# State-space stage: four batches prepared ahead of the state loop, against one unrolled pipeline

## The reference, cut to what matters

```python
xz = _bound(jnp.einsum('bld,ed->ble', hidden_states, W_in))
x, z = jnp.split(xz, 2, axis=-1)
...
x = _bound(jax.nn.silu(jnp.transpose(xc, (0, 2, 1))))      # xc: causal convolution over 4 tokens, plus conv_b
x_dbl = jnp.einsum('bld,ed->ble', x, W_x)                  # 8 columns dt, 16 columns B, 16 columns C
dt = _bound(x_dbl[..., :DT_RANK])
...
dt = jnp.einsum('blr,dr->bld', dt, W_dt) + b_dt
dt = jnp.clip(jax.nn.softplus(dt), 0.0001, 20.0)
def step(h, inp):
    u_t, dt_t, B_t, C_t = inp
    dA = jnp.exp(-dt_t[..., None] * A)
    h = dA * h + (dt_t * u_t)[..., None] * B_t[:, None, :]
    y = jnp.einsum('bdn,bn->bd', h, C_t)
    return (h, y)
y = _bound(jnp.transpose(ys, (1, 0, 2)) + x * D)
y = _bound(y * jax.nn.silu(z))
return jnp.einsum('bld,ed->ble', y, W_out)
```

## Time and profile before

| | us |
|---|---|
| median of 3 runs | 5451.67 (5448.25 to 5453.95) |
| the profiled execution, its own time | 5438.05 |
| its span in the trace | 5436.3 |
| preparation of the four batches, until the first `dtu` | 48.10 to 153.39: 105.29 |
| state loop over the four batches, until the last residual | 153.39 to 487.55: 334.16 |
| the rest: loads and norm ahead, attention stacks and top-k behind | 4996.9 |

### The profile page before, as it was taken

The page is one execution under the profiler, slowest core; times in us unless marked ns, Lnnn a source line. Parts: engine busy times, 40 slices in busy tenths (PEclk is TensorE's granted clock), DMA queues, the critical chain, the costliest instruction groups (busy, mean ns, idle before and its releaser), DMA issues. The chain is left out here.

```text
span 5436.3 us, 135547 instructions
## 1 busy us (share of the span) xinstructions
PE 4737.4 (87%) x51446; PEld 3032.6 (56%) x51638; DVE 4133.6 (76%) x8982; ACT 3352.3 (62%) x7201; POOL 2735.3 (50%) x3646
## 2 busy tenths in 40 slices
PE   4775899999999999777777778658999999999997
PEld 2232566666666666434444344335666666666665
DVE  5897677777777777479898999966777777777774
ACT  2432677777777777444545444435777777777775
POOL 1221666666666666223233333316666666666663
PEclk7898999999999999988888889869999999999999
DMA  0000222222222222100000000002222223222221
GB/s 18 0 0 12 75 71 71 68 69 69 78 62 74 67 76 63 27 15 2 2 2 2 1 2 2 2 1 79 67 73 65 77 62 79 65 74 67 76 63 40
DMA packets 162491, 247.18 MB, mean 45 GB/s; under 512 B 36228, under 2 KB 56640, under 8 KB 161734
## 3 DMA queue, kind: packets, MB, share of 16 engines
q1 hardware_dynamic: 161862, 238.65, 16.9%
HBM read 36.15 MB, written 1.05 MB: 7 GB/s over the span
## 5 line engine op out<-in xcount | busy, mean ns | idle before, releaser
L940 POOL TENSOR_TENSOR f_rope<-f_rope,f_t 128x1024 f32<-128x1024 f32 x384 | 905.7, 2359 | 524.2 <-DVE f_t L854 524.2
L953 POOL TENSOR_TENSOR f_rope<-f_rope,f_rn 128x1024 f32<-128x1024 f32 x384 | 730.6, 1903 | 56.7 <-POOL f_rn L932 2.6
L490 PE MATMUL psum<-f_wqkv,f_xs 128*128 128x512 f32 x1536 | 729.6, 598 | 22.6 <-DVE f_t L854 22.6
L859 DVE TENSOR_REDUCE f_ss<-f_sq 128x16 f32<-128x1024 f32 x384 | 459.9, 1198 | 335.9 <-ACT f_sq L721 333.0
L1827 POOL TENSOR_SCALAR tk_scores<-tk_scores,tk_m 128x408 f32<-128x408 f32 (+28 forms) x232 | 239.2, 1031 | 783.2 <-DVE tk_m L1787 619.3
L684 ACT ACTIVATE f_kT<-psum 64x512 f32<-64x512 f32 (+1 forms) x960 | 485.3, 525 | 83.4 <-PE psum L481 73.8
L721 ACT ACTIVATE f_sq<-psum 128x1024 f32<-128x1024 f32 x384 | 393.3, 1024 | 218.7 <-PE psum L490 218.3
L854 DVE TENSOR_TENSOR f_t<-psum,f_rot 128x1024 f32<-128x1024 f32 x384 | 466.0, 1213 | 0.0
L850 DVE TENSOR_TENSOR f_rope<-psum,f_rot 128x1024 f32<-128x1024 f32 x384 | 465.3, 1212 | 0.0
L876 DVE TENSOR_REDUCE f_den<-f_prob 128x16 f32<-128x1024 f32 x192 | 234.2, 1220 | 296.0 <-ACT f_prob L726 296.0
L490 PEld LDWEIGHTS psum<-f_wqkv,f_xs 128*128 128x128 f32 x1536 | 279.3, 192 | 305.9 <-issue 298.7
(11 more groups left out here) (240 smaller groups left out, 9759.7 us busy)
## 6 DMA issues: line engine op xcount, KB each, us to landing
f_v<-f_v_tok SPq DMA_DIRECT2D x1152, 128.0 KB, 2.4
f_v<-f_v_tok SPq DMA_DIRECT2D x768, 64.0 KB, 2.0
f_wqkv<-in_Wqkv SPq DMA_DIRECT2D x36, 512.0 KB, 4.0
f_wo<-in_Wo SPq DMA_DIRECT2D x12, 512.0 KB, 4.0
f_w<-in_W SPq DMA_DIRECT2D x12, 341.0 KB, 3.3
f_w<-in_W SPq DMA_DIRECT2D x24, 64.0 KB
tk_wkv<-in_Wkv SPq DMA_DIRECT2D x1, 1024.0 KB
out<-y_tok SPq DMA_DIRECT2D x4, 256.0 KB, 2.5
```

The source lines that it names most:

```text
L490: last = pe.matmul(psum[:, n, :], xs[:, j % 2, :], wqkv[:, INNER * which + 512 * n:INNER * which + 512 * (n + 1)], start=True, stop=True)
L859: dve.tensor_reduce(ss[:, H * half:H * (half + 1)], sq[:, half, :, :], AX_X, ALU.add).then_inc(s[f"{name}_ss"], 1)
L940: pool.tensor_tensor(part, part, t2[:, half, :, :], ALU.add).then_inc(s[f"{name}_added"], 1)
L953: pool.tensor_tensor(part, part, rn[:, H * half:H * (half + 1)].unsqueeze(2).to_broadcast([P, H, DH]), ALU.mult).then_inc(s[f"{name}_norme ...
```

## The change

The two blocks become one, without hardware loops. The first batch is prepared alone; after that each step `m` (16 states x 4 batches) does one state for both halves at once, and one piece of the next batch's preparation (`stage(b + 1, n)`) or of the last batch's finish (`finish(b - 1, n)`) is written behind it. In detail:

- VectorE computes `dbu` for both halves in one 128x1024 operation (the B row is broadcast over the halves) and scans both halves in one 128x1024 scan. Column 0 of every `da` is set to 0 once, which restarts the recurrence at the second half; `da` is then computed for 511 columns.
- GpSimd weights both halves in one 128x1024 operation; `weighted` on VectorE is gone. The scan of step m waits for GpSimd of step m-3 (`hs` has three buffers of both halves).
- The convolution moves to TensorE: 4 matmuls for each half with diagonal matrices `taps`, built by 8 small VectorE operations in the weight block.
- Softplus starts on ScalarE (Abs and Relu with the bias, straight from PSUM), then Exp and Ln over both halves; one table set for Exp and Ln is loaded by hand, so ScalarE loads two tables for each batch, both in the step of the Silu.
- PSUM: banks 0, 1 for B, 2, 3 for C, 4, 5 for the sums, 6, 7 for all projections of preparation and finish, which therefore wait for each other.

The core of the diff:

```diff
-                with dve.Fori(0, B) as b:
...
-                    for n in range(DS):
-                        for c in range(CI):
...
-                            dve.tensor_tensor(dbu[:, i % 4, :], dtu[:, c, :], psum[:, n % 2, :], ALU.mult).then_inc(s["b_used"], 1)
-                            if c == 1 and n:
-                                weighted(n - 1)
...
-                            dve.tensor_tensor_scan(hs[:, i % 4, :], da[:, i % 4, :], dbu[:, i % 4, :], 0.0, ALU.mult, ALU.add).then_inc(s["scanned"], 1)
...
+                def stage(b, n):
+                    q = b % 2
+                    if n in (1, 2):
+                        clamp_x(b, n - 1)
+                    if n in (3, 4):
+                        clamp_z(b, n - 3)
+                    if n == 7:
+                        wait("cv_evac", 2 * b + 2)
+                        dve.tensor_scalar(flat(u[:, q, :, :]), flat(conv[:, :, :]), 0.0, 1.0, ALU.max, ALU.min).then_inc(s["u_done"], 1)
+                    if n == 10:
...
+                    if n == 13:
...
+                        dve.tensor_tensor(flat(dt[:, q, :, :]), flat(dt[:, q, :, :]), flat(soft[:, :, :]), ALU.add).then_inc(s["dt_added"], 1)
+                        wait("dt_added", b + 1)
+                        dve.tensor_scalar(flat(dt[:, q, :, :]), flat(dt[:, q, :, :]), 1e-4, 20.0, ALU.max, ALU.min).then_inc(s["dt_done"], 1)
+                    if n == 14:
...
+                        dve.tensor_tensor(flat(dtu[:, q, :, :]), flat(dt[:, q, :, :]), flat(u[:, q, :, :]), ALU.mult).then_inc(s["dtu_done"], 1)
...
+                for n in range(DS):
+                    stage(0, n)
+                for m in range(B * DS):
+                    b, n = divmod(m, DS)
...
+                    wait("b_full", m + 1)
+                    row = psum[:, BC + m % 2, :].unsqueeze(1).to_broadcast([P, CI, N])
+                    dve.tensor_tensor(dbu[:, m % 2, :, :], dtu[:, b % 2, :, :], row, ALU.mult).then_inc(s["b_used"], 1)
+                    wait("b_used", m + 1)
+                    wait("da_done", m + 1)
+                    wait("hc_done", m - 2)
+                    dve.tensor_tensor_scan(flat(hs[:, m % 3, :, :]), flat(da[:, m % 3, :, :]), flat(dbu[:, m % 2, :, :]), 0.0,
+                                           ALU.mult, ALU.add).then_inc(s["scanned"], 1)
+                    if b:
+                        finish(b - 1, n)
+                    if b + 1 < B:
+                        stage(b + 1, n)
...
             @block.gpsimd
             def _(pool):
...
-                        pool.tensor_tensor(hc[:, i % 4, :], hs[:, i % 4, :], c_sb[:, n % 2, :], ALU.mult).then_inc(s["hc0_done"], 1)
...
+                for m in range(B * DS):
+                    pool.wait_ge(s["scanned"], 1 + m + 1)
+                    pool.wait_ge(s["c_copied"], 1 + m + 1)
...
+                    row = c_sb[:, m % 2, :].unsqueeze(1).to_broadcast([P, CI, N])
+                    pool.tensor_tensor(hc[:, m % 2, :, :], hs[:, m % 3, :, :], row, ALU.mult).then_inc(s["hc_done"], 1)
```

More of the change, by code:

```diff
@@ L1069, in _ @@
             def _(dve):
+                dve.memset(da[:, :, :, 0:1], 0.0)
+                dve.wait_ge(load["loaded"], 1 + 16 * 9)
+                dve.tensor_scalar(neg_a[:, :, :], neg_a[:, :, :], 80.0, None, ALU.min).then_inc(load["copied"], 1)
+                for c in range(CI):
+                    for t in range(DC):
+                        dve.tensor_scalar(taps[:, c, t, :], k.ident[:, :], conv_w[:, c, t:t + 1], None, ALU.mult)
                 dve.wait_ge(load["turned"], 1 + 2)
@@ L1100, in _, with wait @@
             def _(pe):
[L1101 to L1105, removed]
-                    for c in range(CI):
-                        last = pe.matmul(psum[0:XD, 4, :], w_xT[:, c, :], batch(u, c, b), start=(c == 0), stop=(c == CI - 1))
-                    last.then_inc(s["xd_full"], 1)
-                    pe.wait_ge(s["xd_evac"], 1 + b + 1)
-                    for c in range(CI):
-                        pe.matmul(psum[:, 5 + c, :], w_dtT[:, c * P:(c + 1) * P], dtr[:, :], start=True, stop=True).then_inc(s["dt_full"], 1)
+                def wait(sem, count):
+                    if count > 0:
+                        pe.wait_ge(s[sem], 1 + count)
@@ new lines, in project_xz, with convolve @@
+                def project_xz(b, c):
+                    if c < 2:
+                        wait("dt_max", 2 * (b - 1) + c + 1)
+                    else:
+                        wait("xz_evac", 4 * b + c - 1)
+                    pe.matmul(psum[:, SIDE + c % 2, :], w_inT[:, c * P:(c + 1) * P], k.XA[:, b, PAD:ROW], start=True, stop=True).then_inc(s["xz_full"], 1)
+                def convolve(b, c):
+                    wait("xz_evac", 4 * b + c + 3)
+                    for t in range(DC):
+                        last = pe.matmul(psum[:, SIDE + c, :], taps[:, c, t, :], xp[:, c, t:t + N], start=(t == 0), stop=(t == DC - 1))
+                    last.then_inc(s["cv_full"], 1)
@@ new lines, in project_out @@
+                def project_out(b):
+                    if b + 2 < B:
+                        wait("cv_evac", 2 * (b + 2) + 1)
+                    else:
+                        wait("dt_max", 2 * (B - 1) + 1)
+                        wait("out_done", b)
+                    wait("yg_done", b + 1)
+                    for c in range(CI):
+                        last = pe.matmul(psum[:, SIDE, :], w_outT[:, c, :], yg[:, c, :], start=(c == 0), stop=(c == CI - 1))
+                    last.then_inc(s["out_full"], 1)
@@ new lines, in _ @@
+                for n in range(DS):
+                    stage(0, n)
+                for m in range(B * DS):
+                    b, n = divmod(m, DS)
+                    if n == 0:
+                        wait("dtu_done", b + 1)
+                    wait("b_full", m + 1)
[8 more added lines that the diff above has]
+                        finish(b - 1, n)
+                    if b + 1 < B:
+                        stage(b + 1, n)
```

312 lines of the change are left out of this document (150 added, 162 removed).

## The result

The changed kernel takes **5376.53 us** (median of 4 runs, 5375.70 to 5377.91); the kernel before, in the same job, 5451.05 (4 runs, 5448.25 to 5453.95). The ratio is **0.9863, 95% interval 0.9846 to 0.9881**. The prediction was 5382, range 5345 to 5422.

The account below looks back on a forecast made before the run. VectorE was taken to bound the state loop, short waits the preparation. Earlier dt (-74.7) and a longer rest (+4.8) net -69.9 us: 5438.05 becomes 5368.2, plus 13.6 to the median gives 5382 us, range 5345 to 5422.

Parts of the forecast that it names:

- dt of the first batch ready at: First batch's preparation: dt ready at 78.7 us, where states begin, instead of 153.39, a gain of 74.7 us.
- 63 steps: State loop after the first scan: 4.74 us a step (0.22 + 2.36 + 2.16), 298.6 us in all.
- pieces between the scans: VectorE's preparation and finish work between scans: 4.2 and 2.3 us a batch, 20 us over three; bounds 0 and 40.
- TensorE and ScalarE late: State loop: these engines delay the scans by 1 us in each of three batches, 3 us; bounds 0 and 10.
- end: After the last scan: last GpSimd weighting, sums, skip addition, clamps, gate and residual take 12.7 us.
- The lead is just used up: TensorE: convolutions in two steps running add 4.3 us, about equal to the B row's 4 us lead.
- a lead of two steps in `da`: ScalarE: the Silu step's extra 7 us of table loads and activations comes under `da` computed two steps ahead.
- Scans not held: Rival for the state loop: long GpSimd operation lets scans through, TensorE binds, about 5326 us; chance 10%.
- Preparation not hidden: Rival: TensorE's convolutions or ScalarE's Silu stop VectorE, half of a batch's 26 us shows, about 5421 us; chance 12%.
- Low clock: Rival: TensorE falls to 1.2 GHz and binds the state loop, +140 us, about 5592 us; chance 5%.
- GpSimd above 2.6: Rival: broadcasting the C row makes GpSimd's fused operation 3.4 us instead of 2.36, no change, 5450 us; chance 3%.
- the fused step alone is slower than the state of before: State loop: a fused step takes 4.74 us against 4.41, 21 us more over 64 states.

Follow-up runs that it names:

- run 1: Changed kernel with the weighting shared again, GpSimd weighting half 0 and VectorE half 1 from PSUM: 5344.93 us, ratio to the kernel before 0.9817.
- run 2: Changed kernel with `dbu` written to PSUM, so the scan has one SBUF input, GpSimd's fused operation kept: 5335.54 us, ratio 0.9799.
- run 4: Kernel before with only the fused weighting, GpSimd weighting both halves in one operation: 5525.39 us, ratio 1.0146.
- run 5: Changed kernel with a channel's four convolution taps spread over two steps instead of one, and later pieces moved back: 5374.75 us, ratio 0.9843.
- Run 9: Changed kernel with the next state's `da` computed on ScalarE ahead of the Silu step, right behind the C row's copy: 5371.24 us, ratio 0.9854.
- run 3: Changed kernel with dt's clamp moved to step n = 14 and `dtu` to n = 15: 5369.25 us, ratio 0.9855.
- run 8: Unaltered changed kernel and the variant with spread taps, both measured again on one chip: ratio 0.9864 and median 5367.95 us (ratio 0.9849).

## Why the prediction was right, and where its sizes were off

The sign, the mechanism and the place of the end came out: last residual forecast near 418, measured 414.3. From dt ready to the end the forecast was 339.0 us and the trace shows 338.9. That agreement is partly luck, since two terms were off by about ten in opposite directions. The 13.6 us that the forecast added, because the profiled execution before was that much quicker than its median, was right to add: what follows the stage took 4948.8 us there and 4961.0 in the profiled execution after, so the two spans alone differ by 61.0 and not by 73.2.

| term | forecast | measured | why |
|---|---|---|---|
| dt of the first batch ready at | 78.7 | 75.4 | `xd` and dt on TensorE at the higher clock |
| to the end of the first scan | 4.7 | 4.8 | |
| 63 steps | 298.6 | 288.5 | 4.58 a step, not 4.74 |
| pieces between the scans | 20 | 18.7 | |
| TensorE and ScalarE late | 3 | 13.2 | the term of the sum that was mis-sized, outside its bounds (0 to 10) |
| end | 12.7 | 13.5 | the last sums |

- **The step.** The mechanism is shown by runs 1, 2 and 4: the scan is held until GpSimd ends. GpSimd took 2.36 and the rest of the scan 2.14, as forecast (2.36, 2.16). What was off is the 0.22 between the scan's end and GpSimd's start, taken over from the 128x512 scans of the earlier trace rows; behind the 128x1024 scans it is 0.08 (77.98 + 2.29 = 80.27, and GpSimd at 80.36). With the 0.02 of the scan that is 0.16 x 63 = 10 us. Why the gap is smaller was not looked into; in run 4, with 128x512 scans, it is again 0.22 (201.60 to 201.82).
- **The pieces.** Clamp 0.36 to 0.40 (forecast 0.40), operation on two SBUF tiles 0.89 (0.94), n = 13 2.74 (2.9), skip additions 0.77 (0.57), but 0.17 in the last finish beside states, where no clamp of x follows them; clamps, dt rows and residual from PSUM nothing, as forecast. The Trainium skill, page "SBUF — State Buffer", section "Who interferes with whom", names `tensor_scalar` among the operations that can contend with GpSimd for the port that the two share. No row of before showed it; n = 13 now does (2.72 held, 0.69 free), and the trace agrees.
- **Lateness.** "The lead is just used up" and "a lead of two steps in `da`" failed. In steps 5 `dbu` waits for a B row behind the taps: 2.0 + 2.3 + 1.9 us over the three batches, and 0.7 at n = 4 of the second. TensorE had the lead in the first of the two steps (4.59 in the first batch) and lost it in the second (6.57); run 5 takes most of this away. In steps 6 the next `da` stands behind the Silu: 1.87 each, 5.6. ScalarE's lead was about one step and not two: `da` of n = 6 ended 5.45 us ahead of its scan (102.03, and the scan at 107.48), and the C row's copy between it and the Silu then waited until 107.08 for TensorE. At n = 10 `da` stands behind the copy of the new rows: 0.22 each, the 0.25 that the prediction named, and 0.7 in all. Together 13.2. Run 9 takes ScalarE's part (steps 6 and 10) away by the order alone.
- **First batch.** The forecast named 3 us that `xd` and dt could be faster "if the clock stays up" and did not take them. From 56 to 75.4 the granted clock was 0.91, against 0.64 in the same place before (56 to 80), and these matmuls took 1.88 and 1.98 instead of 3.63 and 3.78, 3.6 less; the rest from u to dt was 0.7 shorter. Against that u was ready at 64.9 instead of 63.9, because the taps of the weight block did not lie beside the transposes and the first projection started 1.1 later (below). So dt came 3.3 earlier than forecast.
- **End.** The last two sums took 2.90, the two before them 1.98 (forecast 1.97); the granted clock was 0.66 in the last.
- **Rivals.** Scans not held: out by the 3.43 of the scan; run 2 shows what it would have given, 5335 against the forecast 5326. Preparation not hidden: some 8 us of a batch's 26 show (4.0 of pieces and 4.4 of lateness). Low clock: from 78 to 400.8 the granted clock was 0.96. GpSimd above 2.6: it was 2.35 undisturbed. The forecast that the fused step alone is slower than the state of before held: 4.58 against 4.41 in the pipeline, and 5.48 in the old loop, 68 us.

What stays open: why runs of one program meet the low clock at the end of the top-k stage for different lengths (the spread taps have medians of 5374.75 and 5367.95), and with it whether runs 3 and 5 are faster than the change by the whole time. Of the pipeline's parts (the preparation beside the states, one scan over both halves, the taps on TensorE) none was run by itself; the timeline shows that the states begin 78.0 us earlier than before and end 338.9 instead of 334.2 us after that.

## What to carry to other kernels

Before an operation is moved to GpSimd, look at what VectorE does meanwhile: if it reads two SBUF tiles, the two engines take turns, and the longer GpSimd operation can cost more than the VectorE instruction that it saves; one input in PSUM removes the hold. When the preparation of the next block is put between the steps of a loop, price each engine's list for itself: a step has room for a piece only on the engine that has idle time in it, and an instruction that others wait for belongs ahead of the piece, not behind it. A gain of a few microseconds in one stage of a long kernel is read from the trace of the stage, where the clock of the rest moves the whole time by more.

## What was not expected of the hardware

A small clamp in the weight block, 0.25 us in the kernel before, took 3.56 beside GpSimd's selection; timeline of the changed kernel, VectorE and GpSimd:

```profile
42.46 3.83 POOL L1091 TENSOR_SCALAR_AFFINE_SELECT mb_sel<-mb_sel 128x4096 f32<-128x4096 f32 x1
42.77 3.56 DVE L1066 TENSOR_SCALAR mb_neg_a<-mb_neg_a 128x32 f32<-128x32 f32 x1 [5.61 <-DMA mb_vec_nat<-in_D]
...
46.25 1.64 DVE L1069 TENSOR_SCALAR mb_taps<-ident,mb_conv_w 128x128 f32<-128x128 f32 x8
```

It ends at 46.33 with GpSimd's operation (46.29), and the eight taps, which the prediction had beside the transposes, come behind it: the first projection starts at 49.89 instead of 48.75. The other runs of the pipeline, whose weight block is the same, show both orders. In five of the eleven profiled executions the clamp starts behind GpSimd's selection and ends 0.03 to 0.04 after it, with a record of 2.54 to 3.58. In the other six it comes first or together with it and takes 0.18 to 0.53, and then one of the taps, 0.27 each elsewhere, takes 3.85 or 3.86 and ends less than 0.1 behind the selection. So the hold is there in every one of them, and which instruction meets it differs. The first projection starts between 48.43 (run 8, where the selection ends at 45.38) and 50.15 (run 5, 46.56).

The second thing is the price of being second: where a VectorE operation on two SBUF tiles (1.2 us) comes first, GpSimd's record grows by 0.89, and where a clamp (0.67) comes first, by 0.36. In both rows shown GpSimd's growth is 0.15 less than what VectorE's operation has left when GpSimd is recorded to start (144.40 to 145.43, and 146.98 to 147.49), which fits taking turns rather than sharing.
